# Where the first layer's softmax probabilities are divided by their sums: GpSimd or VectorE

## What is computed

```python
x = x + _L0_xattn_ref(_layernorm(x), ctx, mask, W_q, W_k, W_v, W_o, b_o)

sim  = einsum('bihd,bjhd->bhij', q, k) * scale       # 8 heads, 512 tokens, 64 positions
sim  = where(mask, sim, -max)
attn = jax.nn.softmax(sim, axis=-1)                  # over the 64 positions
out  = einsum('bhij,bjhd->bihd', attn, v)
return out @ W_o + b_o
```

## Time and profile before

| | us |
|---|---|
| median of 3 runs | 1735.97 |
| lowest and highest | 1731.9 and 1739.66 |
| the profiled execution, timed | 1736.07 |
| its span, first to last instruction | 1734.3 |
| PE, DVE, ACT, POOL busy | 1346.4, 937.0, 480.5, 327.4 |
| mean granted clock of TensorE | 0.866 of full |

### The profile page before, as it was taken

One profiled execution on the slowest core, in us unless ns is written; L12 is line 12 of the kernel. 1 busy time (PEld: TensorE's weight loads), 2 busy tenths in 40 slices (PEclk: granted clock), 3 DMA queues, 4 the chain that ended last, 5 costly groups with the idle time before them and its releaser, 6 DMA issues. The chain is left out here.

```text
span 1734.3 us, 19407 instructions
## 1 busy us (share of the span) xinstructions
PE 1346.4 (78%) x5358; PEld 815.4 (47%) x5358; DVE 937.0 (54%) x3400; ACT 480.5 (28%) x823; POOL 327.4 (19%) x592
## 2 busy tenths in 40 slices
PE   0265768699789969978987996998887470899997
PEld 0235434354545535454554544556444250567665
DVE  6855315767556557665655656575765527221211
ACT  0432201116203421620432152152241122222221
POOL 3210101103201210320220122032022110433422
PEclk9995779799879959978996996898897685899999
DMA  8000020200020030012002002000200005153511
GB/s 255 1 0 1 2 62 15 59 16 4 14 74 15 12 75 15 0 34 53 15 12 75 15 0 68 19 14 0 75 1 25 1 1 201 44 141 77 142 17 22
DMA packets 44847, 72.33 MB, mean 42 GB/s; under 512 B 8085, under 2 KB 26648, under 8 KB 44634
## 3 DMA queue, kind: packets, MB, share of 16 engines
q1 hardware_dynamic: 38618, 62.90, 12.5%
q0 software_dynamic: 6144, 8.52, 2.8%
HBM read 58.31 MB, written 13.11 MB: 41 GB/s over the span
## 5 line engine op out<-in xcount | busy, mean ns | idle before, releaser
L770 POOL TENSOR_SCALAR ve<-mv 128x2 f32<-128x2 f32 x80 | 18.1, 227 | 897.1 <-DVE mv L868 897.0
L1283 PE MATMUL ps<-x,keys 128*128 128x512 f32 x256 | 137.0, 662 | 11.1 <-DVE hT L954 11.0
L1283 PE MATMUL ps<-zT_second,w 128*128 128x512 f32 x256 | 119.6, 604 | 10.8 <-ACT big L1249 9.4
L1366 PE MATMUL ps<-hT,values 128*128 128x512 f32 x256 | 119.4, 594 | 0.0
L1809 PE MATMUL experts_ps<-experts_yT,experts_fc 128*128 128x512 f32 x256 | 113.4, 602 | 1.3 <-ACT experts_yT L1732 1.3
L1283 PE MATMUL ps<-w,big 128*128 128x256 f32 x512 | 113.6, 381 | 0.8 <-ACT big L1249 0.8
L1821 PE MATMUL experts_ps<-experts_fc,experts_hT 128*128 128x256 f32 x512 | 112.1, 380 | 0.8 <-ACT experts_hT L1744 0.8
L1283 PEld LDWEIGHTS ps<-w,big 128*128 128x128 f32 x512 | 96.8, 190 | 22.5 <-issue 8.5
L1821 PEld LDWEIGHTS experts_ps<-experts_fc,experts_hT 128*128 128x128 f32 x512 | 96.8, 190 | 14.6 <-ACT experts_hT L1744 1.6
L1283 PE MATMUL ps<-vf,amT 65*128 65x512 f32 x128 | 89.9, 819 | 14.1 <-ACT amT L1139 13.2
L437 PE MATMUL pk<-setup_WA,setup_U 128*32 128x16 f32 x512 | 27.9, 214 | 93.5 <-DVE setup_WA L346 93.5
(11 more groups left out here) (382 smaller groups left out, 2598.7 us busy)
## 6 DMA issues: line engine op xcount, KB each, us to landing
gT<-expert_gates SPq DMA_DIRECT2D x16, 1024.0 KB, 9.7
experts_fc<-in_fc1T SPq DMA_DIRECT2D x8, 1024.0 KB, 6.4
experts_fc<-in_fc2T SPq DMA_DIRECT2D x8, 1024.0 KB, 10.1
expert_table<-tb SPq DMA_DIRECT2D x8, 528.0 KB, 12.4
x<-in_x SPq DMA_DIRECT2D x8, 512.0 KB, 3.3
xT<-in_xT SPq DMA_DIRECT2D x8, 512.0 KB, 3.5
out_x<-x SPq DMA_DIRECT2D x8, 512.0 KB, 11.2
w<-in_W SPq DMA_DIRECT2D x2, 1024.0 KB, 13.1
```

The lines of the kernel that those rows point to most:

```text
L770: nc.gpsimd.tensor_scalar(o, i, c, None, ALU.add).then_inc(*tick(*event))
L1283: last = nc.tensor.matmul(o, l, r_, start=start, stop=stop)
L1366: last = nc.tensor.matmul(bank("O2", k), S["values"][:, c, k * P:(k + 1) * P], hT[:, c % RING, :], start=(c == 0), stop=(c == HC - 1))
```

## The change

POOL's stage `attend` is deleted. Its one multiplication is written on DVE instead, in `soften`, right behind the reciprocal that it needs and before the maximum of the next tile. It multiplies the same operands in place and gives the same signal `pr`. The wait for `rs` is now one of DVE on its own result. There are 4 such instructions in each of 8 batches, 32 in all, and nothing else is moved.

```diff
--- before.py
+++ after.py
@@ -786,14 +786,6 @@
-            def attend(b, s):
-                if s:
-                    t = s - 1
-                    probs = e_buf[:, t % 2, :].rearrange("p (h j) -> p h j", h=H0)
-                    g.wait_ge(*at(b, "rs", t))
-                    nc.gpsimd.tensor_tensor(probs, probs, rs[:, t, :].unsqueeze(2).to_broadcast([P, H0, J]),
-                                            ALU.mult).then_inc(*tick("pr", t))
-
@@ -853,7 +845,7 @@
-            trips(g, {"norm": norm_first, "attend": attend, "gates": gates, "rows": rows, "norm_ffn": norm_ffn, "ffn": ffn,
+            trips(g, {"norm": norm_first, "gates": gates, "rows": rows, "norm_ffn": norm_ffn, "ffn": ffn,
                       "norm_out": norm_out, "scores": scores})
@@ -884,6 +876,9 @@
                     nc.vector.tensor_reduce(sm[:, t, :], heads(e_buf[:, t % 2, :], H0), AX, ALU.add).then_inc(*tick("sm", t))
                     v.wait_ge(*at(b, "sm", t))
                     nc.vector.reciprocal(rs[:, t, :], sm[:, t, :]).then_inc(*tick("rs", t))
+                    v.wait_ge(*at(b, "rs", t))
+                    probs = heads(e_buf[:, t % 2, :], H0)
+                    nc.vector.tensor_tensor(probs, probs, rs[:, t, :].unsqueeze(2).to_broadcast([P, H0, J]), ALU.mult).then_inc(*tick("pr", t))
```

## The result

| | before | after |
|---|---|---|
| median, us (5 runs each, side by side) | 1736.2 (1731.9 to 1739.66) | 1745.82 (1743.83 to 1747.85) |
| ratio, 95% interval | | 1.0054 [1.0035, 1.0073] |
| profiled execution, us | 1736.07 | 1745.08 |
| its span, us | 1734.3 | 1743.3 |

The account below looks back on a forecast made before the run. Neither VectorE nor GpSimd was the bound as a whole (TensorE busy 78%), so PE's waits for the product, 30.1 us, counted. From 1736.07 us, +0.7 (batch 0) + 1.2 (batch 1) - 0.9 (rounds) gave 1737.1 us, range 1730 to 1744.

Parts of the forecast that it names:

- forecast 0.42 and 0.24: Rounds of batches 2 to 7: tile 2's product holds `mr` to 0.42 us instead of 0.19, making `x_text` 0.24 late.
- forecast -0.9: Batches 2 to 7: tile 3's shorter product gives -0.39 us, the held `mr` takes back 0.24; six rounds of -0.15.
- the term of +1.9: Batches 0 and 1: VectorE's added work makes their last transposes later, by 0.7 and 1.2 us.
- the wait of 6.04 us: Batch 1: PE's long wait wouldn't shrink, since tile 2 comes 2 us sooner but tile 3, on which all depends, later.
- some 2.4: Rounds: PE's wait before tile 3's transposes would grow from 0.80 to some 2.4 us.
- rival 3: Rounds: DVE becomes the ring's slowest engine, its 0.73 us push landing three times a round, 13.1 us; 1751.1 us, chance 0.04.
- Rival 2: Rounds: PE's 1.74 us wait at tile 2 really goes, 6 x -2.13 = -12.8 us; 1725.2 us, chance 0.05.
- Rival 1: Rounds: VectorE and GpSimd exclude each other by who came first, `mr` 0.48 late, +0.5 us; 1738.5 us, chance 0.2.
- What goes at tile 2 comes back at tile 3: Rounds: PE's 1.74 us wait saved before tile 2's transposes returns before tile 3's, so it was given nothing.
- rival 4: Whole kernel: a delay shifts the granted clock or loop's return, some 4 us either way; beyond 0.5% chance 0.04, half each side.
- After tile 3 all gains and losses pass on unchanged: Rounds, behind tile 3: DVE's extra 0.61 us is free in its 12.24 us wait, and the loop's return just shifts.
- no instruction outside the softmax changes: Sign in the profile: the prediction called itself wrong if an instruction outside the softmax changed its length.

Follow-up runs that it names:

- e10: The changed kernel plus nine useless weight matmuls on PE in tile 3's wait, batches 2 to 7: 1771.22 us, ratio 1.0187.
- e12: The changed kernel plus three useless weight matmuls on PE in tile 3's wait, batches 2 to 7: 1745.88 us, ratio 1.0022.
- e14: The changed kernel plus 5, 3 and 6 useless matmuls in PE's waits at a round's end and three in tile 3's wait: 1738.37 us, ratio 0.999.
- e1: The changed kernel with PE doing the GELU product of chunk 5 twice in every batch: 1745.81 us, ratio 1.0037.
- e3: The kernel before with only tile 3's product moved to VectorE: 1736.38 us, ratio 0.9987.
- e4: The kernel before with the products of tiles 0, 1 and 3 on VectorE, tile 2's left on GpSimd: 1742.32 us, ratio 1.0017.
- e11: The kernel before with only tile 3's product on VectorE, run again later: 1738.18 us, ratio 0.9989.
- e7: The kernel before with tile 3's product on VectorE and 9, 8 and 14 useless matmuls in PE's waits at a round's end: 1787.77 us, ratio 1.0271.
- e13: The kernel before with tile 3's product on VectorE and 5, 3 and 6 useless matmuls in PE's waits at a round's end: 1725.1 us, ratio 0.9907.
- e15: The kernel before, products still on GpSimd, with 5, 3 and 6 useless matmuls in PE's waits at a round's end: 1730.1 us, ratio 0.9919.
- e6: The kernel before with the products of batches 0 and 1 only on VectorE: 1743.69 us, ratio 1.0027.
- c0: The changed kernel itself, run and profiled a second time: 1750.15 us, ratio 1.0056.
- e5: The kernel before with the products of batches 2 to 7 only on VectorE: 1742.9 us, ratio 1.002.
- e9: The changed kernel with eight more register-only instructions on VectorE ahead of batch 1's softmax: 1747.38 us, ratio 1.0044.
- e8: The changed kernel with 9, 8 and 14 useless matmuls in PE's waits at a round's end: 1796.67 us, ratio 1.0323.
- e2: The kernel before with only tile 2's product moved to VectorE: 1751.8 us, ratio 1.0068.

## Why the prediction was wrong

What held. Tile 3's product gives PE 0.39 us a round (20.34 to 19.95). GpSimd's `mr` is held: it starts at 571.62 and takes 0.42 us, ending 0.05 after the product's end (571.30 + 0.69), and `x_text` is 0.23 late; forecast 0.42 and 0.24. The two together are 6 x -0.16, forecast -0.9. In batch 0 the last transposes come 0.68 us later, counted from the first maximum, forecast 0.7; in batch 1 it is 0.84 against 1.2. But only 0.26 and 0.35 of that reach the attention's sum (line 895, 22.17 us after the first maximum instead of 21.91, and 36.00 instead of 35.65), so the term of +1.9 was three times too large: +0.6. That it didn't pass on unchanged worked in the forecast's favour. In batch 1 the wait of 6.04 us, said not to shrink, was parted into 1.89 and 3.50. PE's wait before tile 3 is 2.59 us, where "some 2.4" was expected. DVE's maxima stand where they stood (8.19, 14.29 and 24.70 us after the round's first, before and after), so rival 3 (DVE as the slowest engine) is out. It was closer than forecast: the waits of tiles 1 and 3 shrank from 1.97 and 2.06 us to 1.25 and 1.34, but tile 2's from 1.22 to 0.14, where 0.49 was to be left, with one of the stalls (0.27 us) just ahead of it and a start without a wait in the profile's row (562.92). Rival 2 (tile 2's wait really goes) is out too: PE's total wait went from 30.1 to 30.5 us.

Rival 1, that the two engines exclude each other by who came first, is out by the same rows: the power of 570.83 to 571.54 was under way when the product started at 571.30, the product didn't wait for it, and both took their usual 0.71 and 0.69 us. The Trainium skill, page "SBUF — State Buffer", section "SBUF: two separate sides", says that the first of the two keeps the port for its whole instruction. The held `mr` agrees with that; the product inside the power does not, and the rows decide.

What failed, step by step:

1. **"What goes at tile 2 comes back at tile 3", given nothing.** This is the step that failed for the largest part. As a sum of waits this was right to 0.4 us in 30. It was wrong to price a wait by its length. Two waits of 1.74 and 0.80 us with work between them cost 2.54 us; one of 2.59 cost 2.59 and, in three rounds of six, 1.62 more, as the clock fell. That is 4.9 us of the 9.0 in the profiled pair (6.4 in the second execution, with four falls). The prediction had written down the 2.4 us wait and didn't ask what PE's clock does behind it.
2. **"A shift of granted clock": rival 4, at 0.04, and taken for scatter.** The clock's row on the page seemed to say that it changes anyway. But the falls have a place, and they go when the wait before them is filled. In the last transform of batch 0 the same cost 2.5 us. Eight traces without added work in the tail have VectorE's product of tile 2 in batches 0 and 1: six show 11.7 us there, one 11.5 and one 10.3. The five traces without that product show 9.2 to 9.3. That much is shown; which of PE's waits of batch 1 does it was not tried.
3. **"After tile 3 all gains and losses pass on unchanged", and no instruction outside the softmax changes.** DVE's stream had other instructions in other places, and a stall of 0.28 us, with 0.35 us of delay behind it, got into a chain where it counts: 0.46 us a round, 2.8 in all.
4. **The range.** It took the runs' spread of the old kernel as the bound of what clock and loop's return can do. That spread is of one program; a changed one gets other waits.

PE's wait in the rounds' softmax and the falls behind it, over the profiled executions of this study, one for each kernel:

| the long wait, us | kernels | falls in six rounds | cost of one, us |
|---|---|---|---|
| none, or 0.87 | e10, e12, e14, e1 | 0 | |
| 1.74 and 0.80 or 0.40 | before, e3, e4, e11, e7, e13, e15 | 0 | |
| 2.00 and 0.80 | e6 | 2 | 0.68 |
| 2.59 | after, c0, e5, e9, e8 | 3, 4, 3, 3, 5 | 1.4 to 1.7 |
| 2.98 | e2 | 4 | 1.4 to 3.0 |

The zero of e4 is from the execution with the highest clock of its twelve.

The Trainium skill, page "TensorE: Matmul & The Clock Gate", section "What's actually happening", says that a monitor in the hardware sets the clock by how busy the engine has lately been, on a beat of its own that isn't reset by the kernel. That a long wait brings a fall only sometimes fits such a monitor, and so does that the same program fell in batches 3, 5 and 7 in one execution and 2, 3, 5 and 6 in another.

## What to carry to other kernels

Before moving work off TensorE's path, list its waits before and after by length and not by sum: two short waits that merge into one can slow the matmuls behind them, which no instruction's own row shows until the granted clock is read beside it. Where such a wait can't be broken up, matmuls of no use in it, no longer than the wait, can pay, if their real length is first read from a row. And compare the lengths of instructions that the change doesn't touch: they are where an unforeseen cost shows first.

## What the runs showed of the hardware

- In the rounds' softmax the granted clock fell to half behind some of PE's waits of 2.00, 2.59 and 2.98 us, and, in the profiled executions, behind none of those of 0.40 to 1.76 us. A fall cost 0.7 to 3.0 us, and in which rounds it came changed from one execution to the next.
- Filled waits raised the mean granted clock of the whole kernel from 0.866 to 0.906 and took 16 us off its time, although PE's busy time rose from 1346 to 1385 us.
- VectorE stalls of 0.23 to 0.40 us, for which the profile names no other engine, stand at fixed places of a program: 24 in the change, none before (but six of 0.18), 6, 12 and 18 in variants. With eight instructions added ahead of them the change's 24 were gone, and shorter ones stood some 0.7 us earlier.
- GpSimd's 128x2 multiply that starts while VectorE reads two SBUF tensors ends 0.05 us after it (0.42 us instead of 0.19); a power under way isn't touched (0.71 us).
